# Delta-rule attention and a gated FFN on one core: the Square for the RMS norm moved to GpSimd, with a new order of all engines and of the PSUM pairs

## What is computed

```python
q = _causal_conv_silu(x @ Wq.T, conv_q).reshape(Bx, Tx, H, DK)
k = _causal_conv_silu(x @ Wk.T, conv_k).reshape(Bx, Tx, H, DK)
v = _causal_conv_silu(x @ Wv.T, conv_v).reshape(Bx, Tx, H, DV)
q = _l2_norm(q)
k = _l2_norm(k)
alpha = jnp.exp(-jnp.exp(A_log) * jax.nn.softplus(a_lin + dt_bias))
beta = 2.0 * jax.nn.sigmoid(x @ Wb.T)
...
def step(S, inp):
    q_t, k_t, v_t, a_t, b_t = inp
    kS = jnp.einsum('bhd,bhdv->bhv', k_t, S)
    kkS = jnp.einsum('bhd,bhv->bhdv', k_t, kS)
    S = a_t[..., None, None] * (S - b_t[..., None, None] * kkS) + jnp.einsum('bhd,bhv->bhdv', k_t, v_t)
    o_t = jnp.einsum('bhdv,bhd->bhv', S, q_t)
    return (S, o_t)
...
o = _rms_norm(o).astype(x.dtype).reshape(Bx, Tx, H * DV)
return o @ Wo.T
```

## Time and profile before

| | |
|---|---|
| median of 3 runs | 3353.07 us (3339.13 to 3358.72) |
| the profiled execution | 3340.66 us, its span 3337.6 us |
| mean granted TensorE clock | 0.984 |
| TensorE busy | 2815.5 us (84%) |
| ScalarE busy | 2659.5 us (80%) |
| VectorE busy | 2548.3 us (76%) |
| GpSimd busy | 2050.2 us (61%) |
| DMA | 260.24 MB, mean 78 GB/s |

### The profile page before, as it was taken

One profiled execution on the slowest core, in us unless ns is written; L12 is line 12 of the kernel. 1 busy time (PEld: TensorE's weight loads), 2 busy tenths in 40 slices (PEclk: granted clock), 3 DMA queues, 4 the chain that ended last, 5 costly groups with the idle time before them and its releaser, 6 DMA issues. The chain is left out here.

```text
span 3337.6 us, 200210 instructions
## 1 busy us (share of the span) xinstructions
PE 2815.5 (84%) x80122; PEld 2329.8 (70%) x80122; DVE 2548.3 (76%) x5448; ACT 2659.5 (80%) x5680; POOL 2050.2 (61%) x3422
## 2 busy tenths in 40 slices
PE   6688888888888888888888888888888888888767
PEld 5567777777777777777777777777777777777635
DVE  5677777777777787777777778787877777877656
ACT  3588888888888888888888888888888888888755
POOL 1456666666666666666666666666666666666527
PEclk9799999999999999999999999999999999999979
DMA  2233333333333333333333333333333333333401
GB/s 85 61 79 82 78 82 78 82 78 82 78 82 78 82 78 82 78 82 78 82 78 82 78 82 78 82 78 82 78 82 78 82 78 82 78 82 78 102 23 45
DMA packets 931827, 260.24 MB, mean 78 GB/s; under 512 B 824256, under 2 KB 898240, under 8 KB 931776
## 3 DMA queue, kind: packets, MB, share of 16 engines
q1 hardware_dynamic: 931616, 259.01, 34.5%
q0 software_dynamic: 160, 0.53, 0.0%
HBM read 203.29 MB, written 56.11 MB: 78 GB/s over the span
## 5 line engine op out<-in xcount | busy, mean ns | idle before, releaser
L871 DVE SCALAR_TENSOR_TENSOR cv<-ps,w_v,cv 128x512 f32<-128x512 f32 x768 | 576.7, 751 | 403.1 <-ACT cv L738 385.0
L871 DVE SCALAR_TENSOR_TENSOR cv<-ps,w_kq,cv 128x512 f32<-128x512 f32 x768 | 575.4, 749 | 95.0 <-ACT cv L738 72.7
L529 PE MATMUL ps<-xnT,w_kq 128*128 (+1 forms) x1024 | 300.0, 414 | 111.1 <-DVE cv L871 100.0
L529 PE MATMUL ps<-xnT,w_v 128*128 (+1 forms) x1024 | 298.0, 412 | 82.5 <-DVE cv L871 68.4
L996 POOL TENSOR_TENSOR sc<-tabP,sc 128x8 f32<-128x8 f32 x128 | 26.4, 206 | 491.1 <-DVE sc L886 491.1
L529 PEld LDWEIGHTS ps<-xnT,w_kq 128*128 128x128 f32 x1024 | 173.7, 189 | 189.9 <-issue 169.0
L1031 POOL TENSOR_TENSOR Sg<-S,tabR 128x512 f32<-128x512 f32 x256 | 262.4, 1046 | 69.9 <-DVE S L979 69.9
L1040 POOL TENSOR_TENSOR accT<-accT,X 128x512 f32 (+1 forms) x128 | 163.5, 1277 | 219.5 <-ACT Y L836 219.5
L836 ACT ACTIVATE X<-ps,sc 128x128 f32<-128x128 f32 x512 | 146.3, 368 | 179.2 <-PE ps L725 179.2
L971 DVE SCALAR_TENSOR_TENSOR Rr<-ps,sc,Vt 128x128 f32<-128x128 f32 x1024 | 275.2, 341 | 0.2 <-PE ps L644 0.2
L784 ACT ACTIVATE Vt<-ps,sc 128x128 f32<-128x128 f32 x1024 | 272.4, 363 | 0.8 <-PE ps L589 0.7
(11 more groups left out here) (217 smaller groups left out, 7915.5 us busy)
## 6 DMA issues: line engine op xcount, KB each, us to landing
Lm<-scrD SPq DMA_DIRECT2D x256, 128.0 KB, 2.9
scrN<-Nd SPq DMA_DIRECT2D x256, 128.0 KB, 2.6
ex<-scrG SPq DMA_DIRECT2D x256, 128.0 KB, 2.9
Z<-scrZ SPq DMA_DIRECT2D x256, 128.0 KB, 3.3
X<-scrX SPq DMA_DIRECT2D x512, 64.0 KB
w_kq<-wtab SPq DMA_DIRECT2D x128, 132.0 KB, 2.4
w_v<-wtab SPq DMA_DIRECT2D x128, 132.0 KB, 2.8
wo_s<-wo SPq DMA_DIRECT2D x128, 128.0 KB, 2.5
```

The costliest lines, as they stand in the source:

```text
L529: last = nc.tensor.matmul(pj[:, 4 * g:4 * g + 4, 0:CW], w[:, (j % 2) * P:(j % 2 + 1) * P], xnT3[:, 4 * g:4 * g + 4, bass.ds((n % NC) * C, ...
L871: nc.vector.scalar_tensor_tensor(cv4[:, j], pj[:, :, k:k + C], tap(j, k), cv4[:, j], ALU.mult, ALU.add).then_inc(conv[j].sem, 1)
```

## The change

ScalarE's Square of o, out of PSUM, is removed. GpSimd squares instead ScalarE's copy `oo`, out of SBUF. So the Square now starts when the copy is done, and the copy of the next step has to wait until GpSimd has read `oo`; the copy itself is moved to the pass in which o is made. Besides, the order of the work is a new one on all five engines, and twelve of the seventeen groups in the table of PSUM pairs get another pair.

```diff
-        PB = {"nk": 2, "gk": 4, "nq": 4, "gp": 2, "ktr": 2, "vtr": 4, "y0": 6, "z0": 4, "x": 4, "y1": 6, "z1": 6, "ks": 6, "u": 6, "o": 4, "ds": 6, "ms": 4, "wo": 2}
+        PB = {"nk": 6, "gk": 6, "nq": 6, "gp": 4, "ktr": 2, "vtr": 6, "y0": 4, "z0": 4, "x": 4, "y1": 6, "z1": 2, "ks": 2, "u": 4, "o": 6, "ds": 4, "ms": 6, "wo": 2}
...
-        def act_osq(act, m):
-            act.wait_ge(o_mm.sem, o_mm.at(m))
-            if not first(m):
-                act.wait_ge(ms_mm.sem, ms_mm.at(m - 1))
-            nc.scalar.activation(osq[:], bank(PB["o"], 2), ACT.Square).then_inc(osq_ok.sem, 1)
-
         def act_oc(act, m):
             act.wait_ge(o_mm.sem, o_mm.at(m))
             if not first(m):
                 act.wait_ge(wo_mm.sem, wo_mm.at(m - 1))
+                act.wait_ge(osq_ok.sem, osq_ok.at(m - 1))
             nc.scalar.activation(oo[:], bank(PB["o"], 2), ACT.Copy).then_inc(oc_ok.sem, 1)
...
+        def pool_osq(pool, m):
+            pool.wait_ge(oc_ok.sem, oc_ok.at(m))
+            if not first(m):
+                pool.wait_ge(ms_mm.sem, ms_mm.at(m - 1))
+            nc.gpsimd.tensor_tensor(osq[:], oo[:], oo[:], ALU.mult).then_inc(osq_ok.sem, 1)
+
...
             if n is not None:
                 if m is not None:
-                    pe.wait_ge(conv[3].sem, conv[3].at(m))
+                    pe.wait_ge(conv[1].sem, conv[1].at(m))
                 pe_proj(pe, n, 0)
...
             if n is not None:
                 pool_elim(pool, n)
+                pool_cr(pool, n)
+            if m is not None:
+                pool_osq(pool, m)
```

More of the change, by code:

```diff
@@ L1171, in sp_body @@
         def sp_body(sp, l, m, n):
+            if m is not None:
+                sp_gram_in(sp, m)
             if n is not None:
                 sp_d(sp, n)
-            if l is not None:
-                sp_wo(sp, l)
+                if not first(n):
+                    sp_wv(sp, n)
+                if not first(n):
+                    sp_wkq(sp, n)
             if m is not None:
[L1177 to L1180, removed]
+                sp_x_out(sp, m)
                 sp_z_out(sp, m)
-                sp_x_out(sp, m)
                 sp_z_in(sp, m)
-            if n is not None and not first(n):
-                sp_wv(sp, n)
-            if m is not None:
                 sp_x_in(sp, m)
@@ L1189, in sp_body @@
                 sp_gram(sp, n)
-                sp_gram_in(sp, n)
+                sp_g(sp, n)
+            if m is not None:
+                sp_wo(sp, m)
         def pe_body(pe, l, m, n):
@@ L1215, in pe_body @@
             if n is not None:
[L1216 to L1223, removed]
+                pe.wait_ge(conv[0].sem, conv[0].at(n))
+                pe_proj(pe, n, 2)
                 if l is not None:
@@ L1227, in pe_body @@
                     pe.wait_ge(v_ok.sem, v_ok.at(m))
+                pe_nk(pe, n)
+                pe.wait_ge(n2_ok.sem, n2_ok.at(n))
                 pe_gram_k(pe, n)
+            if m is not None:
+                pe.wait_ge(pt_ok.sem, pt_ok.at(m))
+                pe_y(pe, m, 0)
             if l is not None:
[L1230 to L1235, removed]
+                if m is not None:
+                    pe.wait_ge(r0_ok.sem, r0_ok.at(m))
+                    pe.wait_ge(r1_ok.sem, r1_ok.at(m))
                 else:
-                    pe.wait_ge(pt_ok.sem, pt_ok.at(l))
+                    pe.wait_ge(z_ok.sem, z_ok.at(l))
                 pe_wo(pe, l)
             if m is not None:
+                pe_z(pe, m, 0)
+            if n is not None:
+                pe.wait_ge(conv[2].sem, conv[2].at(n))
+                pe_proj(pe, n, 3)
+            if m is not None:
+                pe_x(pe, m)
                 if n is not None:
@@ L1266, in pe_body @@
                 else:
-                    pe.wait_ge(n2_ok.sem, n2_ok.at(n))
+                    pe.wait_ge(r0_ok.sem, r0_ok.at(m))
+                    pe.wait_ge(r1_ok.sem, r1_ok.at(m))
+                pe_z(pe, m, 1)
+            if n is not None:
+                pe.wait_ge(conv[3].sem, conv[3].at(n))
+                pe_proj(pe, n, 1)
+            if m is not None:
+                pe.wait_ge(x_ok.sem, x_ok.at(m))
+                pe_u(pe, m, 1)
+                pe.wait_ge(x_ok.sem, x_ok.at(m))
+                pe_u(pe, m, 0)
+            if n is not None:
+                if m is not None:
+                    pe.wait_ge(z_ok.sem, z_ok.at(m))
                 pe_ktr(pe, n)
@@ L1348, in dve_body @@
             if m is not None:
+                dve_s(dve, m, 1)
                 dve_s(dve, m, 0)
-                dve_s(dve, m, 1)
+            if n is not None:
+                dve_k(dve, n)
         def pool_body(pool, l, m, n):
```

90 lines of the change are left out of this document (35 added, 55 removed).

## The result

The changed kernel took 3402.64 us, the median of 4 runs (3393.08 to 3414.37), beside 3346.45 for the kernel before in 4 runs. The ratio is 1.016, 95% interval 1.013 to 1.019: slower by 1.6%, where the prediction said 2.4% (3425) and had 3335 to 3460 as its range. The profiled execution took 3394.37 us, its span 3392.5. The four runs of the kernel before lie two by two, near 3339.5 and at 3353.07 and 3358.72, so the 56 us between the medians can be off by some 10 us either way, as the interval says.

What follows compares the result with a forecast made beforehand. No single engine bounds the kernel; the order of passes does. The longer of two loops, Z's DMA loop at 24.44 us against 23.80, adds 0.64 times 127, 81 us, to 3340.7: 3422, stated as 3425, range 3335 to 3460.

Steps and rivals of the forecast that it cites:

- The DMA loop: Z's write to memory and read back between passes, through TensorE and ScalarE: 24.44 us a pass, 0.64 above before; chance 0.44.
- TensorE's loop: Chain from k projection through V copies, Wo, taps and U to the next k projection: 24.03 us a pass, 0.23 more.
- Part 1: Square moved from ScalarE to GpSimd: removal hidden by k projection and transposes, price 0, with 0.1 us as high end.
- the cover that I had called thin: On GpSimd, D behind the Square, ready near 4.3 us; its ScalarE reader is free at 4.4, so 0.1 us cover.
- Part 2: New order on TensorE and ScalarE, laid out step by step: U starts at 17.75 us, a pass takes 24.03.
- Part 3: DMA queue: Z's write now waits behind XB's, so its landing is no longer hidden; loop 24.44 us a pass.
- part 4: VectorE's S, K and tap passes, GpSimd's elimination, other PSUM pairs: readers 0.3 to 0.6 us later than their ends; price 0.
- TensorE's loop alone: Rival: Z lands sooner than 3.8 us after first issue, pass 24.03 us, run about 3370, up to 3390; chance 0.24.
- No change: Rival: with Z landing early, TensorE's loop comes out within 0.5%, 17 us, of before: 3324 to 3357; chance 0.11.
- faster: Rival: ScalarE's work was the bound; a pass loses the Square's 0.92 us: 3224, or about 3300 for a third; chance 0.13.
- Slower still: Rival: XB's data hold up Z's, or D behind the Square holds up ScalarE: 24.7 to 25.1 us, 3455 to 3500; chance 0.08.

Runs made afterwards that it cites:

- both edits: The changed kernel with Z's write issued ahead of X's and U's halves in the old order 0 then 1: 3367.87 us, ratio 1.0047 to the kernel before.
- the run with less of R: The changed kernel with Z's write ahead of X's and three of four instructions of R's half 0 on VectorE left out: 3355.23 us, ratio 1.0009.

## Why the prediction was right, and where it was off

**The direction, and the mechanism.** The Square was given price 0, and alone, in the old order, it measured none. The 1.6% come from the new order, and from the two loops that the prediction laid out: with Z's write ahead of XB's only TensorE's is left, at 24.12 us a pass where 24.03 was forecast; with it behind, the median pass is 24.25, in the forecast's 24.2 to 24.6, at its low end. The weights were other than forecast. The DMA loop was to set every pass, 0.41 above TensorE's; it adds 0.13 in the median, and most of the 0.41 us that a pass has grown, 0.28, is TensorE's loop. The time, 3402.64, is in the range and 22 us under the predicted one; the step up is 56 us where 81 were forecast.

**Part 1.** The price was right, the cover in part. The part says that ScalarE waits for transposes ahead of the V copies, and names these and the k projection as what hides the Square. In the kernel before, these copies start at 1506.44 behind XB's (1505.91 and 0.63 long), without a wait; what hid the Square is the k projection alone, for which ScalarE waits ahead of the first tap, and in the run with the Square alone that wait took up its time (0.23 to 1.14). The Square took 1.89 us and not 2.1, and began 0.18 after the k projection, as soon as the copy of o was done, so it ended at 2.07. The part has its end at 2.6 to 2.8, while its own terms, 0.1 and 2.1 to 2.3, add up to 2.2 to 2.4. Timeline of GpSimd, in the pass of the table below:

```profile
1504.53 1.89 POOL L1011 TENSOR_TENSOR KB<-oo 128x1024 f32<-128x1024 f32 x1 [2.60 <-ACT oo L822]
1506.38 1.04 POOL L982 TENSOR_TENSOR Lm<-Lm,tabP 128x512 f32<-128x512 f32 x1
```

D follows without the 0.5 us that the turn of the loop had been given. So D was made 3.1 after the k projection, not near 4.3, and the cover that I had called thin was 1.2 us.

**Part 2, step by step** (us after the k projection at 1504.35, forecast and measured):

| step | forecast | measured |
|---|---|---|
| V copies start | 2.40 | 2.22 |
| mean-square group | 4.67 | 4.54 |
| k norm | 6.83 | 6.73 |
| Wo | 9.18 | 9.24 |
| scaled copies | 11.37 | 11.39 |
| tap of v1 | 13.47 | 13.41 |
| U | 17.75 | 17.73 |
| next k projection | 24.03 | 24.13 |

The rows of VectorE's timeline on which this rests answer to the earlier trace rows:

```profile
1512.04 0.20 DVE L881 RECIPROCAL sc<-sc 128x8 f32<-128x8 f32 x1
1512.22 1.13 DVE L966 SCALAR_TENSOR_TENSOR Rr<-ps,sc,Vt 128x128 f32<-128x128 f32 x4
```

and those of ScalarE's to the earlier trace rows:

```profile
1506.57 2.18 ACT L784 ACTIVATE Vt<-ps,sc 128x128 f32<-128x128 f32 x8 [0.24 <-PE ps L589]
...
1515.74 1.14 ACT L831 ACTIVATE X<-ps,sc 128x128 f32<-128x128 f32 x4 [1.01 <-PE ps L725]
...
1517.76 0.74 ACT L738 ACTIVATE cv<-ps,w_v 128x512 f32<-128x512 f32 x1
```

The V copies started 0.18 sooner than the step took, since XB's copy and the tap ahead of them are done by then and only the transposes count; Wo lost that again, with 2.51 from the k norm and not 2.35. The one step that failed is its last sentence, that from U to the next k projection nothing changes: it is 6.40 and not 6.28, and the run with U's halves in the old order gives 0.11 of it back. The new order makes U's halves in the other order, and the step did not price that.

**Part 3.** The mechanism held, the size was off in three terms. From SyncE's and TensorE's timelines over all passes, in the median, Z's write to the read is 2.56 and not 2.88, and the read to a first reader that waits for it 4.03 and not 4.22; in the pass shown, one issue of scrX ahead of Z's 0.85 (1529.81 to 1530.66) and not 0.66. With these three, and 2.97 in place of 2.85 from U to the output, the sum is 24.24, 0.12 above TensorE's loop and not 0.41; the read's scatter (to the reader 3.9 to 4.2 in most passes) then puts one loop ahead or the other. The three longest passes have a third cause: XB's copy itself late, behind the inverses of the blocks, which part 4 had put at nothing. Timeline of ScalarE in the pass whose Y group waits 0.72:

```profile
848.41 0.66 ACT L857 ACTIVATE XB<-XT 64x256 f32<-64x256 f32 x1 [0.36 <-DVE XT L945]
```

By the fit of the Trainium skill's page "DMA: Bandwidth & Descriptors" (section "Anatomy of one DMA — SWDGE (gpsimd) path"), which is for DMAs that GpSimd issues, 2.3 us for 128 KB as an estimate, this loop would not bind. Z's DMAs are issued by SyncE, and the trace has 4.03 after the change and 4.22 before it, from the first issue to the reader.

**The rivals.** *TensorE's loop alone* is not the changed kernel, but the kernel with Z first, whose 3387.43 us are inside what this rival gave as its time. The sign that was to tell it from the forecast, a first Y group that waits for the DMA of Z, tells little: the kernel before has it in 97 passes. *No change* and *faster* failed where the prediction said: the V copies started at 2.22 and not at 1.9, since they wait for transposes (0.24) and not for ScalarE's queue, and Wo started at 9.24 and not before 8.6. *Slower still* failed too: the issue ahead of Z's cost 0.85, most of which was in the sum, and D had 1.2 us of cover. Freed time on ScalarE did bring a gain elsewhere, 0.7%, but only together with the move of the table load out of the way of Z; either edit alone brought none.

What stays open: the 0.5% that are left of the new order with both edits. TensorE's loop is 24.02 us there against 23.84 before. By the sum it is the mean-square group waiting for V's copies and Wo waiting for R, and the run with less of R bears out the second (0.24 a pass); the first is argued from the rows alone, since no run put the projection back into its old place in the new order.

## What to carry to other kernels

Lay a new order out as a sum of rows, for TensorE and for the DMA queue apart, and compare the loops: here two were within 0.15 us a pass, and a swap of two lines in the queue was worth 0.6%. Do not take a row of waits for a price: 96 waits for Z in the old order, with their 39.3 us, were worth nothing that the time could tell, and 79 with 29.8 us were worth 0.6% in the new one. Ask of every group that moves what its old place was hiding: with the q projection ahead of it, V copies 0.5 us late moved the mean-square group by 0.25; in the new order, V copies 0.7 late moved it by 0.66. Where halves are made in another order, look at the reader that still waits for the old first one: here it was 0.11 us a pass.

## What the runs showed of the hardware

TensorE waits for U's half 0 and then for half 1. The idle time ahead of the output matmuls is 0.54 us where half 0 comes last and 0.43 where half 1 does, with the same copies. Why it is so was not tried.

GpSimd's product of a tensor with itself takes 1.89 us for 1024 columns; its products of two different full tensors take 1.27 for 512. The forecast of 2.1 was from the one row with the same tensor twice, 1.04 for 512.

A small product on GpSimd, 8 columns, takes 0.73 us where it runs beside VectorE's product of two SBUF tensors, and 0.21 in the place that it had before. Timeline of VectorE:

```profile
1501.18 0.68 DVE L935 TENSOR_TENSOR tmpS<-NS,XT 64x512 f32<-64x512 f32 x1
```

and of GpSimd:

```profile
1501.20 0.73 POOL L999 TENSOR_TENSOR sc<-tabR,sc 128x8 f32<-128x8 f32 x1
```

It ends 0.07 us after VectorE's. So it is in 116 of the 128 steps, where it starts 0.02 to 0.03 us behind VectorE's product; in the other 12, where it starts ahead of it, it takes 0.20, in this place too. The Trainium skill's page "SBUF — State Buffer" (section "Who interferes with whom") has it that a VectorE instruction with two SBUF inputs and a GpSimd one that reads SBUF keep each other out; the trace agrees for the second of the two to start. No reader of the product shows a wait for it.
